# Norms of a 12-sublayer decoder: means summed on TensorE, squares' means in column tiles, inverses on 100 columns

## The reference

```python
def _layernorm(x, axis=-1, eps=1e-05):
    m = jnp.mean(x, axis=axis, keepdims=True)
    v = jnp.var(x, axis=axis, keepdims=True)
    return (x - m) / jnp.sqrt(v + eps)
```

## Time and profile before

| | us |
|---|---|
| median of 3 runs | 3539.7 |
| lowest, highest | 3533.76, 3539.82 |
| the profiled execution, its own time | 3534.41 |
| its span, first to last instruction | 3532.6 |
| TensorE busy | 3000.9 (85%) |
| VectorE busy | 1560.5 (44%) |
| ScalarE busy | 1036.7 (29%) |
| mean granted TensorE clock | 0.914 |

### The profile page before, as it was taken

The page is one execution under the profiler, slowest core; times in us unless marked ns, Lnnn a source line. Parts: engine busy times, 40 slices in busy tenths (PEclk is TensorE's granted clock), DMA queues, the critical chain, the costliest instruction groups (busy, mean ns, idle before and its releaser), DMA issues.

```text
span 3532.6 us, 36213 instructions
## 1 busy us (share of the span) xinstructions
PE 3000.9 (85%) x14276; PEld 1880.4 (53%) x14276; DVE 1560.5 (44%) x2609; ACT 1036.7 (29%) x2982; POOL 469.2 (13%) x494
## 2 busy tenths in 40 slices
PE   7889989998889999789598989999787877999951
PEld 4445454554655565467354555555444455777740
DVE  5510277103835555410365656566365667000026
ACT  3210161101723333212172223223135441444420
POOL 0000000000000000022201212120010001555555
PEclk9889989999899999899798999999798867999985
DMA  3011102100011110179300010011000002999964
GB/s 149 17 44 42 60 15 70 43 29 1 17 36 45 43 47 30 48 283 326 95 24 11 31 45 32 19 39 36 24 18 22 1 1 77 368 361 366 364 216 116
DMA packets 78377, 319.04 MB, mean 90 GB/s; under 512 B 13408, under 2 KB 13408, under 8 KB 66432
## 3 DMA queue, kind: packets, MB, share of 16 engines
q0 software_dynamic: 39264, 186.30, 15.0%
q1 hardware_dynamic: 16880, 90.19, 7.2%
q10 hardware_dynamic: 22064, 40.25, 3.1%
HBM read 274.80 MB, written 41.88 MB: 90 GB/s over the span
## 4 chain that ended last, share of the span: by engine, by line
PE 71%; DVE 17%; ACT 7%; issue 3%; POOL 2%; DMA 1%; POOLq 0%; ACTq 0%; SPq 0%; DVEq 0%
PE P L878 32%; PE P L880 14%; PE P L1199 9%; PE P L1097 3%; PE P L1079 3%; ACT A L1314 3%; PE P L886 3%; DVE A L1475 2%; PE P L891 2%; DVE A L1916 1%; POOL A L2000 1%; DVE A L1727 1%; DVE A L1725 1%; DVE A L1726 1%; ACT A L1431 1%
## 5 line engine op out<-in xcount | busy, mean ns | idle before, releaser
L878 PE MATMUL P<-A,W 128*128 128x400 f32 (+1 forms) x1888 | 691.4, 506 | 10.3 <-DVE A L1755 6.8
L1246 ACT ACTIVATE A<-P 128x400 f32<-128x400 f32 (+5 forms) x770 | 411.8, 543 | 969.1 <-PE P L880 452.3
L878 PEld LDWEIGHTS P<-A,W 128*128 128x128 f32 x1888 | 362.5, 195 | 283.9 <-issue 33.7
L2000 POOL DMA_INDIRECT A<-experts,A x141 | 134.3, 952 | 2010.2 <-DVE A L1901 1855.3
L886 PE MATMUL P<-C,A 128*128 128x128 f32 (+4 forms) x1553 | 230.4, 273 | 163.1 <-DVE A L1925 130.6
L878 PE MATMUL P<-X,W 128*128 128x400 f32 x864 | 336.6, 528 | 34.4 <-DVE X L1579 30.1
L1199 PEld LDWEIGHTS P<-A 128*128 128x128 f32 x2704 | 328.6, 194 | 69.2 <-issue 41.0
L1199 PE MATMUL P<-A 128*128 128x128 f32 x2704 | 329.6, 277 | 1.4 <-ACT A L1246 1.4
L886 PEld LDWEIGHTS P<-C,A 128*128 128x128 f32 (+4 forms) x1553 | 181.8, 149 | 206.1 <-DVE A L1925 140.1
L1916 DVE TENSOR_TENSOR A<-P,A 128x128 f32<-128x128 f32 (+1 forms) x141 | 44.9, 318 | 552.9 <-ACT A L1431 552.9
L878 PEld LDWEIGHTS P<-X,W 128*128 128x128 f32 x864 | 170.1, 201 | 165.6 <-DVE X L1579 34.1
(11 more groups left out here) (230 smaller groups left out, 3746.1 us busy)
## 6 DMA issues: line engine op xcount, KB each, us to landing
W<-weights SPq DMA_DIRECT2D x60, 1024.0 KB, 4.8
slot_outputs<-A ACTq DMA_DIRECT2D x141, 256.0 KB
W<-weights SPq DMA_DIRECT2D x32, 448.0 KB, 3.4
x_by_token<-A ACTq DMA_DIRECT2D x16, 200.0 KB
A<-experts,A POOLq DMA_INDIRECT x141
A<-x_by_token,A POOLq DMA_INDIRECT x141
W<-weights SPq DMA_DIRECT2D x8, 256.0 KB, 2.6
C<-constants SPq DMA_DIRECT2D x1, 1990.5 KB, 17.2
```

The source lines that it names most:

```text
L878: self.e.matmul(out, a, b, start=i == 0, stop=False)
L1246: self.e.activation(out, in_, ACT.Copy).then_inc(*self.of(*item))
L2000: self.e.indirect_dma_start(out, None, table, bass.IndirectOffsetOnAxis(ap=idx, axis=0)).then_inc(sem, 16)
```

## The change

- The mean is taken by three matmuls that add up in PSUM: one over the sum of blocks 0 and 1, which VectorE makes ahead (`norm_pair`, 400 columns, put between the second and third projection of the half), one over block 2, one over block 3 (`norm_mean`). `norm_mean` is a step of its own.
- The subtraction is four operations of 400 columns, the square four as well, each with its own semaphore count.
- The squares' mean (`moment`) is taken by 16 matmuls with 32 weight columns: block m, columns 100j to 100j+99, into partitions 32j to 32j+31 of one bank, added up over m. VectorE's sums of the squares go. The bank then holds 128 partitions x 100 columns: each token's value 32 times.
- Square root and reciprocal run on 128x100. `widen` then spreads them by four matmuls with a 128x128 matrix that has one row of ones (row 32j) into 128x400 of a further bank, and the multiplication reads that bank.
- In `norms()` the `None` goes. The list beside the o-projection of half 1 is now: projection 0, mean, projection 1, centre, pair of half 1, scale, projection 2, projection 3 (`out`).
- In `mla` `norm_pair` stands behind the second back-projection, and half 0's three steps beside latent, back 0 and back 1. In `moe` pair and mean of half 0 stand behind the fourth combination, centre and scale behind the fifth.
- The widening matrices (512 columns) join the first constants, which are then 1044 columns; two tables of counts (64 and 113 columns) become views of another. Two arena areas move (the rms result of sublayer 2, the rope's temporary of sublayer 3).

```diff
+    e = np.zeros((128, 4, 128), np.float32)
+    for j in range(4):
+        e[32 * j, j, :] = 1.0
+    c["widen"] = e.reshape(128, -1)
...
+        self.first = sum(self.consts[n].shape[1] for n in ("mean", "eps", "restart", "widen"))
+        self.c["iota"], self.c["tiles"] = self.c["slots"][:, 0:64], self.c["slots"][:, 0:113]
...
+        c.PAIR = c.RS[:, H2:T]
...
     def norms(self, c):
-        return [[("norm_add", c, h), ("norm_centre", c, h), None, ("norm_scale", c, h)] for h in range(2)]
+        return [[("norm_mean", c, h), ("norm_centre", c, h), ("norm_scale", c, h)] for h in range(2)]
+
+    def out(self, c, h, side=()):
+
+        steps = [("proj", c.o, m, h) for m in range(4)]
+        steps.insert(2, ("norm_pair", c, h))
+        yield from beside(steps, side)
...
         first, tail = self.norms(c)
-        yield from self.projection(c.o, ([], first))
+        yield from self.out(c, 0)
+        yield from self.out(c, 1, first)
...
-        side = [("proj", c.o, m, 0) for m in range(4)]
+        side = [[("proj", c.o, m, 0)] for m in range(4)]
+        side[1].append(("norm_pair", c, 0))
         for t, steps in pipeline(("scores", "exps", "shares", "turn", "values"), c):
             yield from steps
             if t < len(early):
                 yield from early[t]
             if t >= NB and side:
-                yield side.pop(0)
-        yield from side
+                yield from side.pop(0)
+        for steps in side:
+            yield from steps
         first, tail = self.norms(c)
-        yield from self.projection(c.o, ([], first), (1,))
+        yield from self.out(c, 1, first)
...
-            return [("latent", c, g, half)] + [("back", c, g, m, half) for m in range(4)]
+            steps = [("latent", c, g, half)] + [("back", c, g, m, half) for m in range(4)]
+            return steps[:3] + [("norm_pair", c, half)] + steps[3:] if g == 3 else steps
...
-        first = [("norm_add", c, 0), ("norm_centre", c, 0), ("norm_scale", c, 0)]
+        first, tail = self.norms(c)
+        first[0:1] = [("norm_pair", c, 0), first[0]]
         for b in range(NB):
             for j in range(c.kk):
                 yield "collect", c, b, j
             yield "combine", c, b
             if b in (3, 4, 5):
-                yield first.pop(0)
-        return [("norm_add", c, 1), ("norm_centre", c, 1), ("norm_scale", c, 1)]
+                yield from first[:2]
+                first = first[2:]
+        return [("norm_pair", c, 1)] + tail
...
-    def mean(self, SQ, h, *job):
-        self.e.matmul(self.ps(*job)[:, 0:H2], self.c["mean"], SQ[:, 0, hs(h)], start=True, stop=True).then_inc(*self.of(*job))
+    def moment(self, SQ, h, sq, *job):
+
+        P = self.ps(*job)
+        for m in range(4):
+            self.wait_ge(self.at(*sq, m))
+            for j in range(4):
+                at = H2 * h + S * j
+                i = self.e.matmul(P[32 * j:32 * j + 32, 0:S], self.c["mean"][:, 0:32], SQ[:, m, at:at + S], start=m == 0, stop=m == 3)
+        i.then_inc(*self.of(*job))
+
+    def widen(self, RS, h, *job):
+
+        P = self.ps(*job)
+        w = v4(self.c["widen"])
+        for j in range(4):
+            i = self.e.matmul(P[:, ss(j)], w[:, j, :], RS[:, ss(h)], start=True, stop=True)
+        i.then_inc(*self.of(*job))
 
     def rms_sc(self, c, w, h):
-        self.take(("mean", "rms", w, h), ("std", "rms", w, h))
+        self.take(("moment", "rms", w, h), ("std", "rms", w, h))
         self.wait_ge(self.at("consts"))
-        self.wait_ge(self.at("sum", "rms", w, h))
-        self.mean(c.SQ, h, "mean", "rms", w, h)
+        self.moment(c.SQ, h, ("sq", "rms", w, h), "moment", "rms", w, h)
+        self.take(("widen", "rms", w, h), ("xn", w, h))
+        self.wait_ge(self.at("inverse", "rms", w, h))
+        self.widen(c.RS, h, "widen", "rms", w, h)
+
+    def norm_mean(self, c, h):
+        P = self.take(("mean", c.n, h), ("centred", c.n, h, 3))
+        self.wait_ge(self.at("pair", c.n, h))
+        for item in self.k.z_ready(c, h):
+            self.wait_ge(self.at(*item))
+        self.chain(P[:, 0:H2], [(self.c["mean"], a) for a in (c.PAIR, c.Z[:, 2, hs(h)], c.Z[:, 3, hs(h)])], "mean", c.n, h)
 
     def norm_centre(self, c, h):
-        self.take(("mean", "mean", c.n, h), ("centred", c.n, h))
-        self.wait_ge(self.at("sum", "mean", c.n, h))
-        self.mean(c.SQ, h, "mean", "mean", c.n, h)
+        self.take(("moment", "norm", c.n, h), ("std", "norm", c.n, h))
+        self.moment(c.SQ, h, ("sq", "norm", c.n, h), "moment", "norm", c.n, h)
 
     def norm_scale(self, c, h):
-        self.take(("mean", "var", c.n, h), ("std", "norm", c.n, h))
-        self.wait_ge(self.at("sum", "var", c.n, h))
-        self.mean(c.SQ, h, "mean", "var", c.n, h)
+        self.take(("widen", "norm", c.n, h), ("x", c.n, h))
+        self.wait_ge(self.at("inverse", "norm", c.n, h))
+        self.widen(c.RS, h, "widen", "norm", c.n, h)
...
-        self.e.activation(c.SQ[:, :, hs(h)], c.rms[w][0][:, :, hs(h)], ACT.Square).then_inc(*self.of("sq", "rms", w, h))
+        for m in range(4):
+            self.e.activation(c.SQ[:, m, hs(h)], c.rms[w][0][:, m, hs(h)], ACT.Square).then_inc(*self.of("sq", "rms", w, h, m))
 
     def rms_sc(self, c, w, h):
-        self.wait_ge(self.at("mean", "rms", w, h))
-        P = self.ps("mean", "rms", w, h)
-        self.e.activation(c.RS[:, hs(h)], P[:, 0:H2], ACT.Sqrt, bias=self.c["eps"][:, 0:1]).then_inc(*self.of("std", "rms", w, h))
+        self.wait_ge(self.at("moment", "rms", w, h))
+        P = self.ps("moment", "rms", w, h)
+        self.e.activation(c.RS[:, ss(h)], P[:, 0:S], ACT.Sqrt, bias=self.c["eps"][:, 0:1]).then_inc(*self.of("std", "rms", w, h))
...
-        self.wait_ge(self.at("centred", c.n, h))
-        self.e.activation(c.SQ[:, :, hs(h)], c.Z[:, :, hs(h)], ACT.Square).then_inc(*self.of("sq", "norm", c.n, h))
+        for m in range(4):
+            self.wait_ge(self.at("centred", c.n, h, m))
+            self.e.activation(c.SQ[:, m, hs(h)], c.Z[:, m, hs(h)], ACT.Square).then_inc(*self.of("sq", "norm", c.n, h, m))
 
     def norm_scale(self, c, h):
-        self.wait_ge(self.at("mean", "var", c.n, h))
-        P = self.ps("mean", "var", c.n, h)
-        self.e.activation(c.RS[:, hs(h)], P[:, 0:H2], ACT.Sqrt, bias=self.c["eps"][:, 1:2]).then_inc(*self.of("std", "norm", c.n, h))
+        self.wait_ge(self.at("moment", "norm", c.n, h))
+        P = self.ps("moment", "norm", c.n, h)
+        self.e.activation(c.RS[:, ss(h)], P[:, 0:S], ACT.Sqrt, bias=self.c["eps"][:, 1:2]).then_inc(*self.of("std", "norm", c.n, h))
...
-    def sums(self, SQ, src, h, *item):
-
-        self.e.tensor_tensor(SQ[:, 0:2, hs(h)], src[:, 0:2, hs(h)], src[:, 2:4, hs(h)], ALU.add).then_inc(*self.of("pair", *item))
-        self.wait_ge(self.at("pair", *item))
-        self.e.tensor_tensor(SQ[:, 0, hs(h)], SQ[:, 0, hs(h)], SQ[:, 1, hs(h)], ALU.add).then_inc(*self.of("sum", *item))
-
     def inverse(self, RS, h, *item):
-        self.e.reciprocal(RS[:, hs(h)], RS[:, hs(h)]).then_inc(*self.of("inverse", *item))
-        self.wait_ge(self.at("inverse", *item))
-
-    def rms_sq(self, c, w, h):
-        self.wait_ge(self.at("sq", "rms", w, h))
-        self.sums(c.SQ, c.SQ, h, "rms", w, h)
+        self.e.reciprocal(RS[:, ss(h)], RS[:, ss(h)]).then_inc(*self.of("inverse", *item))
 
     def rms_sc(self, c, w, h):
         self.wait_ge(self.at("std", "rms", w, h))
         self.inverse(c.RS, h, "rms", w, h)
         src, dst = c.rms[w]
-        self.e.tensor_tensor(dst[:, :, hs(h)], src[:, :, hs(h)], bc(c.RS[:, hs(h)], [128, 4, H2]), ALU.mult).then_inc(*self.of("xn", w, h))
+        self.wait_ge(self.at("widen", "rms", w, h))
+        P = self.ps("widen", "rms", w, h)
+        self.e.tensor_tensor(dst[:, :, hs(h)], src[:, :, hs(h)], bc(P[:, 0:H2], [128, 4, H2]), ALU.mult).then_inc(*self.of("xn", w, h))
...
-    def norm_add(self, c, h):
+    def norm_pair(self, c, h):
+        if h:
+            self.wait_ge(self.at("mean", c.n, 0))
+        for item in self.k.z_ready(c, h, 1):
+            self.wait_ge(self.at(*item))
+        self.e.tensor_tensor(c.PAIR, c.Z[:, 0, hs(h)], c.Z[:, 1, hs(h)], ALU.add).then_inc(*self.of("pair", c.n, h))
+
+    def norm_centre(self, c, h):
         for item in c.ahead:
             self.wait_ge(self.at(*item))
-        self.wait_ge(self.z_ready(c, h))
-        self.sums(c.SQ, c.Z, h, "mean", c.n, h)
-
-    def z_ready(self, c, h):
-        if c.n in (4, 7):
-            return self.at("back", c.n, 3, 3, h)
-        if c.n in (5, 11):
-            return self.at("z", c.n, 4 * h + 3)
-        return self.at("ev", ("o", c.n), 3, h)
-
-    def norm_centre(self, c, h):
-        Z = c.Z[:, :, hs(h)]
-        self.wait_ge(self.at("mean", "mean", c.n, h))
-        P = self.ps("mean", "mean", c.n, h)
-        self.e.tensor_tensor(Z, Z, bc(P[:, 0:H2], [128, 4, H2]), ALU.subtract).then_inc(*self.of("centred", c.n, h))
-        self.wait_ge(self.at("sq", "norm", c.n, h))
```

(12 more changed lines are left out.)

28 lines of the change are left out of this document (17 added, 11 removed).

## The result

| | before | after |
|---|---|---|
| median (us) | 3536.7 | 3569.5 |
| lowest, highest | 3530.1, 3539.8 | 3568.6, 3571.0 |
| ratio, 95% interval | | 1.0096 (1.0078 to 1.0113) |
| profiled span, mean granted clock | 3532.6, 0.914 | 3566.8, 0.924 |

The change made the kernel 33 us slower by the medians, 34 by the ratio and by the spans. The forecast was 3541 with a range up to 3559: wrong, and the result lies above the range.

What follows compares the result with a forecast made beforehand. TensorE, busy 85% of the span, was taken as the bound, with idle time at the norms. 77.6 us inserted against 62.8, 1.5, 2.5, 2.5 and 7.5 saved gave 3535.4 profiled, forecast median 3541, range 3524 to 3559.

Steps and rivals of the forecast that it cites:

- Insertion: O-projection of half 1, eight sublayers: waits, longer mean and slow clock add 9.7 us each, 77.6 in all.
- Savings elsewhere: Passages between sublayers save 62.8 us; back-projections 1.5 and 2.5, last norm 2.5, sublayer 0 7.5.
- 3 to 4: Passage from sublayer 3 to 4: 23.3 us becomes 13.3 with the chain all exposed, saving 10.0.
- 5 to 6: Passage from sublayer 5 to 6: half 0 gains about 1 us, half 1 loses as much; 0, within 2.
- 10 to 11: Passage from sublayer 10 to 11: 27.1 us becomes 12.8 (four router steps, mean, chain), saving 14.3.
- the last norm: Final norm: 15.4 us becomes 12.9, with its mean at half clock, saving 2.5.
- rival 2: Clock pays twice: half rate lasts longer after eight o-projection waits and follows five passages' waits; 18 us more, 3559; chance 0.28.
- the slow restart: Sublayer 0, second stretch: TensorE's slow resumption after idling for the gate (2.1 us) was expected to go.
- The signs of being wrong: TensorE waiting under 3 us between projections 1 and 2 (then faster), or clock falling where it was 1.00 (then slower).
- Rival 1: Clock holds in the eight o-projection waits because the moments' matmuls break them up; 16 us less, 3525; chance 0.20.
- Rival 4: The moments' column tiles don't run side by side, in about 24 exposed places; 12 us more, 3553; chance 0.05.
- Rival 3: Chain decides: TensorE finds the widening nearly ready, o-projection insertion falls to 2.7 us; 56 less, 3485; chance 0.07.

Runs made afterwards that it cites:

- e10_fill_all: The change plus throwaway matmuls in TensorE's waits: half 0's norm in the eight o-projections, half 1's norms except the last, two rms norms; 3534.6 us, ratio 0.9994.
- e9_moe_apart: The change with half 0's centre and scale each behind its own combination in the two mixtures of experts, as before; 3561.1 us, ratio 1.0069.
- e2_engines: The change with subtraction and squares issued in the mean's step, root and reciprocal in the moments' step, TensorE's order kept; 3484.2 us, ratio 0.9870.
- e3_engines_gap: e2_engines plus the free turn restored before the widening, and the mixtures' centre and scale apart; 3465.3 us, ratio 0.9811.
- e11_single: e3_engines_gap with one subtraction and one square of 1600 columns in place of four and four; ratio 0.9897.

## Why the prediction was wrong, step by step

- **Insertion, 9.7 in eight places (77.6)**: the mechanism was right, and the prices on VectorE and ScalarE too; 10.5 measured (202.3 - 118.5 = 83.8). Mis-sized: the widening itself runs at half clock. From its first record to projection 2 it took 1.82 (389.87 to 391.69), and I had taken 0.68 of issue at full rate. 6.2 us in all.
- **Savings elsewhere, 76.8 (62.8 + 1.5 + 2.5 + 2.5 + 7.5)**: 49.5 measured, (3371.8 + 34.7) - (3313.5 + 43.5). 27.3 us. The rows below run from the evacuation of projection 3 of half 1 of a sublayer to that of projection 0 of half 1 of the next one (in 4, 5, 7 and 11, which have no such projection, to x of half 0). The last column is what e10_fill_all gave back to the change.

| us | forecast | saved | back by fillers |
|---|---|---|---|
| start to o-projection of 0 | 7.5 | 4.5 | 2.2 |
| 0 to 1 | 7.1 | 4.9 | -0.3 |
| 1 to 2 | 4.2 | 1.5 | 3.5 |
| 2 to 3 | 4.2 | -0.1 | 0.1 |
| 3 to 4 | 10.0 | 7.9 | 2.3 |
| 4 to 5, and 5 to 6 | 1.5 | 1.0 | 2.6 |
| 6 to 7 | 11.3 | 10.1 | 2.4 |
| 7 to 8 | 2.5 | 3.4 | 3.2 |
| 8 to 9 | 3.5 | -0.2 | -1.3 |
| 9 to 10 | 8.2 | 5.3 | 1.5 |
| 10 to 11, and the end | 16.8 | 11.2 | 3.1 |

The passages with nothing to hide behind were close where I had priced them: 3 to 4 runs from 999.18 to 1012.46, 13.3 (13.3), 10 to 11 from 2921.93 to 2934.77, 12.8 (12.8), the last norm from 3548.02 to 3561.10, 13.1 (12.9). What failed lies beside them:

- **Sublayer 11, unsaid.** I priced only its last norm. Half 0's centre and scale now stand behind one combination, and I didn't ask what is queued behind the scale step's new wait on VectorE: the sums, and GpSimd's gathers behind them. The row is 5.6 short, and e9_moe_apart gives 6.7 back in it. "5 to 6: 0, within 2" held (4 to 6 is 0.5 short), though sublayer 5 has the same queue and e9_moe_apart gives 2.9 there.
- **The clock inside the attentions of 3 and 9, taken as unchanged.** 3.4 and 2.7 us in the rows 2 to 3 and 8 to 9, as shown above. Nothing in the forecast had a place for it.
- **The clock in the waits of the passages and in sublayer 0.** I had put it into rival 2 (18 us: "1.2 more eight times, and the two waits of half 1 in five passages"), not into the forecast. Fillers there gave back 19 in all. Sublayer 0's second stretch alone has two slow spells of six matmuls (one of them above), 1.7 us each; there I had even counted the slow restart as gone. The gated unit starts at 101.69 against 105.14, 3.4 earlier, not 10.
- **Rival 2 was near the result, in part by luck**: 3559 plus the 9.5 that no case had is 3568.5, measured 3569.5. But its terms were others: 1.2 more in each o-projection (0.8 measured, so its condition, "from about 1 us extra in each place", was just missed), and 8.5 in the five passages that have cover (0 to 1, 1 to 2, 2 to 3, 8 to 9, 9 to 10), where fillers gave back 3.5; the rest of their 19 lies in the bare passages and at the start. I gave it 0.28 because no row of before had gaps like the new ones. The trace had them: 3.57 us ahead of 872.05 and 1.76 ahead of 856.12, both followed by full clock. The passages with a mean clock of 0.68 to 0.81 pointed the other way, and I had written that down as evidence for it.
- **The signs of being wrong**: TensorE's wait between projections 1 and 2, 3.9, isn't under 3. The granted clock did fall where it was 1.00 (872.05 before, 890.06 after), and that sign said slower.
- **Rival 1** (clock holds): the opposite was seen. **Rival 4**: no; 32 records of the moments take 0.89 (382.08 in e2_engines), as in L997's row. **Rival 3** (the chain decides, 3485): wrong for this order, but it says what the arithmetic can do once the order lets it; e3_engines_gap is at 3465. That e2_engines is at 3484 is luck: its o-projections still take 39 more than before, and rival 3 had 8 x 2.7.
- A sum of the prices is off by little: the items of the new chain add up to 7.2 and 7.8, not 7.4 and 7.9.
- The rule on smaller instructions (the Trainium skill, Perfetto Trace Analysis, Optimizing Scalar/DVE Operations) was weighed rightly: by itself it gave no gain in the change; with nothing queued in front of the pieces e11_single shows them worth 28 us.

The miss is 33.5 us of span (6.2 + 27.3). Of the 27.3, some 6 are shown to be the clock inside the attentions and some 6 the held gathers (with 5 us of scatter in that row). 3.0 stand at the start, within its scatter. The other 12.6 are spread over the remaining rows. Fillers gave back more than that in these rows together, but not row by row, so that the clock in the waits makes up these 12.6 is likely and not shown.

## What to carry to other kernels

Where a chain hops between engines, ask for each hop what the engine has queued in front of it, and issue each step's work with the step that feeds it, ahead of evacuations whose matmuls aren't done: that alone was worth 80 us here (e2_engines against the change). Where the change adds a wait, ask the same of what is queued behind it, up to the gathers of another engine. Price a wait on TensorE as its length plus the half-rate matmuls that may follow, and expect the clock to change in stretches that the edit doesn't touch (3.4 and 2.7 us here); where no useful work fits, throwaway matmuls gave 36 us in a kernel with many waits and 14 in one with few.

## What was not expected of the hardware

- A wait of 2.24 us was followed by half clock over the next six matmuls (3.85 against 2.18; granted clock 0.55), a wait of 3.57 in the kernel before by full clock (six in 2.28), and the same wait after the change, 3.56, by half clock (3.28). In the o-projection of sublayer 0 the clock was at 0.50 through the widening and the first matmuls behind it.
- The table load doesn't wait with the root that needs it: it ran at 374.04, the root at 383.04. Where ScalarE reaches it early, it is free; the change had it between squares and root.
